# Attention phase of a four-phase layer: side work laid out tile by tile, projections split in two matmuls, head gather in six transfers with 8 KB runs

## What is computed

```python
def poincare_fully_connected(x, z, r, c):
    lam = 2.0 / (1.0 - c * sum(x * x, axis=-1))
    z_norm = maximum(norm(z, axis=0), EPS)
    inner = x @ (z / z_norm)
    v = 2.0 * z_norm / sqrt(c) * arcsinh(sqrt(c) * lam * inner * cosh(2cr) - (lam - 1.0) * sinh(2cr))
    w = sinh(sqrt(c) * v) / sqrt(c)
    return w / (1.0 + sqrt(1.0 + c * sum(w * w, axis=-1)))

xn = layernorm(x)                       # B=8 rows, T=1024, D=256
Q = poincare_fully_connected(xn, z_q, b_q, 1.0)
K = poincare_fully_connected(xn, z_k, b_k, 1.0)
V = xn @ w_v.T + b_v
probs = softmax(Qh @ Kh.T / 4)          # 16 heads of 16 columns
x = x + probs @ Vh
```

## Time and profile before

| what | value |
|---|---|
| median of 3 runs | 3177.55 us (3175.37 to 3177.95) |
| profiled execution, its own time | 3171.44 us |
| its span in the profile | 3169.6 us |
| mean granted TensorE clock | 0.962 of full |
| busy: PE, ACT, DVE, POOL | 2838.4, 2026.5, 1846.0, 1273.0 us |
| exponentials of `phase_b`, first and last start | 1449.0 and 2769.2 us |

### The profile page before, as it was taken

One profiled execution on the slowest core, in us unless ns is written; L12 is line 12 of the kernel. 1 busy time (PEld: TensorE's weight loads), 2 busy tenths in 40 slices (PEclk: granted clock), 3 DMA queues, 4 the chain that ended last, 5 costly groups with the idle time before them and its releaser, 6 DMA issues. The chain is left out here.

```text
span 3169.6 us, 38539 instructions
## 1 busy us (share of the span) xinstructions
PE 2838.4 (90%) x12161; PEld 1226.5 (39%) x12161; DVE 1846.0 (58%) x2420; ACT 2026.5 (64%) x2650; POOL 1273.0 (40%) x786
## 2 busy tenths in 40 slices
PE   3899999999979999657999999999999999969997
PEld 1455555555554444322323232323233332234443
DVE  8899999999973453454443444444444441144444
ACT  6454555455425555325889797978878889835554
POOL 4798899889861220141314131322313230021210
PEclk7899999999999999778999999999999999989999
DMA  2010001010012211206263635535553627231112
GB/s 80 1 37 27 30 26 36 23 33 26 24 56 75 80 53 53 67 11 132 29 146 42 134 54 94 93 73 92 92 94 58 116 46 128 27 114 48 60 53 67
DMA packets 163998, 200.30 MB, mean 63 GB/s; under 512 B 16504, under 2 KB 118272, under 8 KB 163840
## 3 DMA queue, kind: packets, MB, share of 16 engines
q1 hardware_dynamic: 163840, 198.25, 28.4%
HBM read 139.49 MB, written 58.72 MB: 63 GB/s over the span
## 5 line engine op out<-in xcount | busy, mean ns | idle before, releaser
L1859 ACT ACTIVATE b_pr<-b_ps 128x1024 f32<-128x1024 f32 x1024 | 1002.8, 1025 | 255.5 <-PE b_ps L1956 251.2
L1956 PE MATMUL b_ps<-b_st 128*128 128x512 bf16 x2048 | 591.2, 386 | 71.0 <-DMA b_st<-b_scratch 31.6
L1938 PE MATMUL b_acc<-b_pr,b_vaug 128*32 128x512 f32 x4096 | 549.0, 608 | 0.4 <-ACT b_pr L1859 0.4
L1956 PEld LDWEIGHTS b_ps<-b_st 128*128 128x128 bf16 x2048 | 150.3, 98 | 649.5 <-ACT b_pr L1859 381.9
L1257 PE MATMUL f_po<-f_s,f_w 128*128 128x512 f32 x768 | 355.0, 605 | 9.4 <-DVE f_xr L1042 5.9
L1030 DVE TENSOR_TENSOR f_turned<-f_cs,f_s 128x1024 f32<-128x1024 f32 x96 | 119.3, 1243 | 364.4 <-ACT f_cs L1159 359.4
L635 PE MATMUL a_pv<-a_xnT,a_wv 128*128 128x512 f32 x512 | 251.2, 614 | 52.8 <-DVE a_mem L403 38.7
L1123 ACT ACTIVATE f_h<-f_po,f_b 128x512 f32<-128x512 f32 x192 | 131.9, 687 | 218.1 <-PE f_po L1257 218.1
L627 PE MATMUL a_pu<-a_xnT,a_wk 128*128 128x512 f32 x512 | 238.3, 609 | 29.2 <-DVE a_frac L355 23.2
L1575 POOL TENSOR_TENSOR b_SQ<-b_A 128x1024 f32<-128x1024 f32 x32 | 64.7, 2021 | 467.1 <-DVE b_A L1672 467.1
L674 PE MATMUL a_py<-a_wo,a_out 128*128 128x256 f32 x960 | 229.1, 382 | 0.0
(11 more groups left out here) (259 smaller groups left out, 4694.4 us busy)
## 6 DMA issues: line engine op xcount, KB each, us to landing
b_st<-b_scratch SPq DMA_DIRECT2D x512, 128.0 KB, 7.0
b_scratch<-b_parts SPq DMA_DIRECT2D x32, 768.0 KB, 7.7
f_xl<-x SPq DMA_DIRECT2D x16, 1024.0 KB, 5.5
f_xr<-x SPq DMA_DIRECT2D x16, 1024.0 KB, 6.8
a_xl<-in_L_attn_a_x_dram SPq DMA_DIRECT2D x16, 512.0 KB, 4.2
x<-a_xr SPq DMA_DIRECT2D x32, 256.0 KB, 2.2
x<-f_xr SPq DMA_DIRECT2D x8, 1024.0 KB, 4.5
b_xl<-x SPq DMA_DIRECT2D x8, 1024.0 KB, 7.8
```

What stands on the lines that cost most here:

```text
L1859: nc.scalar.activation(pr[:, 4 * (blk % 2) + j, :], ps[:, j % 2, :], ACT.Exp, scale=SC).then_inc(S["probs_done"], 1)
L1938: x = nc.tensor.matmul(acc[32 * j:32 * j + 32, h * 512:(h + 1) * 512], vaug[:, kt, c:c + 32], pr[:, 4 * (kt % 2) + j, h * 512:(h + 1) * 51 ...
L1956: x = nc.tensor.matmul(ps[:, j % 2, h * 512:(h + 1) * 512], st[:, g % 2, 1, j, kt * P:(kt + 1) * P], st[:, g % 2, 0, j, h * 512:(h + 1) * ...
```

## The change

- **Layout of side work.** The table names single tiles with the unit after which they stand. Two-tile kinds (`inT`, `lamb`, `facb`, `out`) are split in their halves, which may stand in different blocks. A projection tile becomes `proja` and `projb`, one matmul each, after units 0 and 2. ACT steps carry a unit too, and are mostly one to a block. Preparations for the row after next (`stats`, `rstd`, `lam`, `inT`, `lamb` and projection tile 0) now stand in blocks 10 to 31 of the row before; `PROLOGUE` gains those of row 1, and `lam` has a buffer of its own (`dgl`).
- **Order of Q and K columns.** ScalarE permutes the weights once (`zp`), so that a partition of Q or K is (g, d, j) and not (g, j, d); the biases are loaded in that order in eight transfers instead of four.
- **Gather.** `b_scratch` is laid out as [Q or K, part, g, d, j, T]. Each gather is six transfers with 8 KB runs in place of sixteen with 2 KB runs: for Q one part repeated 3, 3 and 2 times (a broadcast of the source), for K parts 0 to 2, 0 to 2 and 0 to 1. The store keeps 2 KB runs.
- **Order on SP.** The load of `xl` comes first in a row, ahead of the gather of group 1.

```diff
-Q_PART = [0, 0, 0, 1, 1, 1, 2, 2]
-K_PART = [0, 1, 2, 0, 1, 2, 0, 1]
+Q_RUNS = [(0, 3, 0), (3, 3, 1), (6, 2, 2)]
+K_RUNS = [(0, 3, 0), (3, 3, 0), (6, 2, 0)]
...
 STEPS = {
-    1: [("inT", 0, 1)],
-    2: [("out", 3, -1), ("inT", 1, 1)],
-    3: [("lamb", 0, 1)], 4: [("proj", 0, 1), ("proj", 1, 1), ("vaug", 3, 0)], 5: [("proj", 2, 1)], 6: [("square", 0, 1), ("proj", 3, 1)],
-    7: [("root", 0, 1), ("y", 0, 1), ("v", 0, 1)], 8: [("ln", 0, 1), ("square", 1, 1), ("proj", 4, 1)],
-    9: [("up", 0, 1), ("root", 1, 1), ("y", 1, 1), ("proj", 5, 1)],
-    10: [("out", 0, 0), ("down", 0, 1), ("v", 1, 1)],
-    11: [("sign", 0, 1), ("ln", 1, 1), ("square", 2, 1), ("proj", 6, 1)],
-    12: [("up", 1, 1), ("root", 2, 1), ("y", 2, 1), ("proj", 7, 1)], 13: [("down", 1, 1), ("v", 2, 1)],
-    14: [("sign", 1, 1), ("ln", 2, 1), ("square", 3, 1), ("v", 3, 1)],
-    15: [("up", 2, 1), ("root", 3, 1), ("y", 3, 1), ("v", 4, 1), ("pair", 0, 1)],
-    16: [("down", 2, 1), ("v", 5, 1)], 17: [("sign", 2, 1), ("ln", 3, 1), ("up", 3, 1), ("sum", 0, 1)],
-    18: [("out", 1, 0), ("down", 3, 1)], 19: [("sign", 3, 1)], 20: [("pair", 1, 1), ("v", 6, 1)],
-    21: [("sum", 1, 1)], 22: [("fac", 0, 1), ("v", 7, 1)], 23: [("facb", 0, 1), ("split", 0, 1)],
-    24: [("facb", 1, 1)], 25: [("split", 2, 1)], 26: [("out", 2, 0)], 27: [("split", 1, 1), ("vaug", 0, 1)],
-    28: [("split", 3, 1), ("stats", 0, 2)], 29: [("vaug", 1, 1), ("rstd", 0, 2)], 30: [("lam", 0, 2)], 31: [("vaug", 2, 1)]}
+    0: [("proja", 1, 1, 0), ("projb", 1, 1, 2)], 1: [("proja", 2, 1, 0), ("projb", 2, 1, 2)],
+    2: [("square", 0, 1, 0), ("proja", 3, 1, 0), ("projb", 3, 1, 2)],
+    3: [("root", 0, 1, 0), ("proja", 4, 1, 0), ("y", 0, 1, 0), ("projb", 4, 1, 2)],
+    4: [("square", 1, 1, 0), ("ln", 0, 1, 2), ("proja", 5, 1, 0), ("vaug", 3, 0, 0), ("projb", 5, 1, 2)],
+    5: [("root", 1, 1, 0), ("up", 0, 1, 2), ("proja", 6, 1, 0), ("y", 1, 1, 0), ("projb", 6, 1, 2)],
+    6: [("square", 2, 1, 0), ("down", 0, 1, 2), ("proja", 7, 1, 0), ("projb", 7, 1, 2)],
+    7: [("ln", 1, 1, 0), ("out", 6, -1, 0), ("out", 7, -1, 2)],
+    8: [("root", 2, 1, 0), ("sign", 0, 1, 0), ("v", 0, 1, 0), ("y", 2, 1, 0)],
+    9: [("up", 1, 1, 0), ("v", 1, 1, 0)],
+    10: [("square", 3, 1, 0), ("v", 2, 1, 0), ("stats", 0, 2, 0)],
+    11: [("down", 1, 1, 0), ("v", 3, 1, 0), ("rstd", 0, 2, 0)],
+    12: [("ln", 2, 1, 0), ("v", 4, 1, 0), ("sign", 1, 1, 0)],
+    13: [("root", 3, 1, 0), ("v", 5, 1, 0), ("y", 3, 1, 0), ("out", 0, 0, 2), ("lam", 0, 2, 0)],
+    14: [("up", 2, 1, 0), ("v", 6, 1, 0), ("pair", 0, 1, 0), ("out", 1, 0, 2)],
+    15: [("down", 2, 1, 0), ("v", 7, 1, 0)], 16: [("ln", 3, 1, 0), ("sum", 0, 1, 0), ("sign", 2, 1, 0)], 17: [("up", 3, 1, 0)],
+    18: [("down", 3, 1, 0), ("out", 2, 0, 2)], 19: [("sign", 3, 1, 0), ("out", 3, 0, 2)],
+    20: [("pair", 1, 1, 0), ("sum", 1, 1, 2)], 21: [("fac", 0, 1, 0)],
+    22: [("facb", 0, 1, 0), ("facb", 1, 1, 2)], 23: [("facb", 2, 1, 0), ("split", 0, 1, 0)], 24: [("facb", 3, 1, 0)],
+    25: [("inT", 0, 2, 0), ("split", 2, 1, 0)], 26: [("inT", 1, 2, 0), ("out", 4, 0, 2)],
+    27: [("inT", 2, 2, 0), ("vaug", 0, 1, 0), ("out", 5, 0, 2)], 28: [("inT", 3, 2, 0), ("split", 1, 1, 0)],
+    29: [("lamb", 0, 2, 0), ("vaug", 1, 1, 0)], 30: [("lamb", 1, 2, 0), ("split", 3, 1, 0)],
+    31: [("proja", 0, 2, 0), ("projb", 0, 2, 2), ("vaug", 2, 1, 0)]}
...
-UNIT_OF = {1: (2,), 2: (0, 2), 3: (0, 1, 3), 4: (0, 1, 2, 3)}
-N_TILES = {"inT": 2, "lamb": 2, "proj": 1, "v": 1, "sum": 1, "facb": 2, "out": 2}
+    "stats0 rstd0 lam0 inT0 inT1 inT2 inT3 lamb0 lamb1 proja0 projb0 proja1 projb1 square0 proja2 projb2 proja3 projb3 "
...
+    [(step[:-1], int(step[-1]), 1) for step in "inT0 inT1 inT2 inT3 lamb0 lamb1 proja0 projb0".split()]
+TILE_KINDS = ("inT", "lamb", "projb", "v", "sum", "facb", "out")
+PE_KINDS = TILE_KINDS + ("proja",)
+ACT_KINDS = ("square", "root", "ln", "up", "down")
...
-    scratch = nc.dram_tensor("b_scratch", [2, 3, D, T], BF16, kind="Internal").ap()
+    scratch = nc.dram_tensor("b_scratch", [2, 3, H // 4, DK, 4, T], BF16, kind="Internal").ap()
...
+        zp = s.sb("zp", [P, 2, KD, D])
...
+        dgl = s.sb("dgl", [P, NT, P])
...
-        N_W = 16 * 8
-        N_G = 16 * 16
...
+        N_W = 16 * 12
+        N_G = 16 * (len(Q_RUNS) + len(K_RUNS))
...
-                sp.dma_start(scratch[o, :, f * P:(f + 1) * P].rearrange("w p t -> p w t"), parts[:, o, :, f, :])\
+                sp.dma_start(scratch[o, :, 2 * f:2 * f + 2].rearrange("w g d j t -> (g d j) w t"), parts[:, o, :, f, :])\
...
-            for o, part in enumerate((Q_PART, K_PART)):
-                for i, w in enumerate(part):
-                    sp.dma_start(st[i * DK:(i + 1) * DK, slot, o],
-                                 scratch[o, w, 64 * g:64 * g + 64, :].rearrange("(h d) t -> d h t", d=DK))\
-                        .then_inc(st_loaded[slot], 16)
+            for i, n, w in Q_RUNS:
+                sp.dma_start(st[i * DK:(i + n) * DK, slot, 0].rearrange("p h t -> p (h t)"),
+                             scratch[0, w, g].rearrange("d h t -> d (h t)").unsqueeze(0).broadcast_to([n, DK, 4 * T]))\
+                    .then_inc(st_loaded[slot], 16)
+            for i, n, w in K_RUNS:
+                sp.dma_start(st[i * DK:(i + n) * DK, slot, 1].rearrange("p h t -> p (h t)"),
+                             scratch[1, w:w + n, g].rearrange("w d h t -> w d (h t)")).then_inc(st_loaded[slot], 16)
...
-                    for f in range(KD):
-                        sp.dma_start(rcol[:, 2 * o + f:2 * o + f + 1],
-                                     r[f * P:(f + 1) * P].rearrange("(p o) -> p o", o=1)).then_inc(S["w_loaded"], 16)
+                    for g in range(G):
+                        c = 2 * o + g // 2
+                        sp.dma_start(rcol[g % 2 * 64:g % 2 * 64 + 64, c:c + 1],
+                                     r[64 * g:64 * g + 64].rearrange("(j d) -> d j", d=DK),
+                                     allow_slow_non_contiguous=True).then_inc(S["w_loaded"], 16)
...
+                    if left > 1:
+                        sp.wait_ge(S["inT_done"], b + 2)
+                        sp.sem_inc(passed, 1)
+                        sp.dma_start(xl[:], dram(xi, b + 2)).then_inc(S["xl_loaded"], 16)
...
-                    if left > 1:
-                        sp.wait_ge(S["inT_done"], b + 2)
-                        sp.sem_inc(passed, 1)
-                        sp.dma_start(xl[:], dram(xi, b + 2)).then_inc(S["xl_loaded"], 16)
...
+                        nc.gpsimd.tensor_tensor(dgl[:], eye, lam.unsqueeze(2).broadcast_to([P, NT, P]), ALU.mult)\
                             .then_inc(S["dlam_done"], 1)
...
+                nc.scalar.activation(zp[:].rearrange("p o k (g d j) -> p (o k g) d j", g=G, d=DK),
+                                     z_sb[:].rearrange("p o k (g j d) -> p (o k g) d j", g=G, d=DK), ACT.Copy).then_inc(S["z_done"], 1)
...
-                        steps = [x for x in steps_at(blk, first, left) if x[0] in ("square", "root", "ln", "up", "down")]
                         for j in range(4):
-                            for kind, i, off in steps[j // 2:j // 2 + 1] if j % 2 == 0 else ():
-                                step(kind, i, b + off)
+                            for kind, i, off, at in steps_at(blk, first, left):
+                                if kind in ACT_KINDS and at == j:
+                                    step(kind, i, b + off)
                             n = 4 * BLK * b + 4 * blk + j
...
-                    if kind == "proj":
...
+                    if kind in ("proja", "projb"):
+                        k = 0 if kind == "proja" else 1
+                        if k == 0:
+                            bank_free(m)
+                            if i == 0:
+                                pe.wait_ge(S["misc_taken"], m - 2)
                         q, c = i // 2, slice((i % 2) * 512, (i % 2 + 1) * 512)
-                        for k in range(KD):
-                            x = nc.tensor.matmul(bank, z_sb[:, q // 2, k, (q % 2) * P:(q % 2 + 1) * P], xnT[:, k, c],
-                                                 start=k == 0, stop=k == KD - 1)
+                        x = nc.tensor.matmul(bank, zp[:, q // 2, k, (q % 2) * P:(q % 2 + 1) * P], xnT[:, k, c],
+                                             start=k == 0, stop=k == KD - 1)
+                        if k == 0:
+                            return
                     if kind == "v":
                         bank_free(m)
                         for k in range(KD):
...
-                            for q, (kind, i, off, h) in enumerate(tiles):
-                                if UNIT_OF[len(tiles)][q] == j:
+                            for kind, i, off, at in steps_at(blk, first, left):
+                                if kind in PE_KINDS and at == j:
                                     if kind == "out":
-                                        out(G * (b + off) + i, m - h, par - h, h)
```

(64 more changed lines are left out.)

108 lines of the change are left out of this document (51 added, 57 removed), and 5 rows, old and new, of the table PROLOGUE.

## The result

| | before | after |
|---|---|---|
| median, same chip | 3176.46 us (3174.16 to 3177.95, 4 runs) | 3320.99 us (3314.82 to 3323.33, 4 runs) |
| ratio | | 1.0453, 95% interval 1.0435 to 1.0471 |
| span of the profiled execution | 3169.6 us | 3318.8 us |
| exponentials, first and last start | 1449.0 and 2769.2 us | 1474.1 and 2918.3 us |

A forecast was written before the change was run, and what follows sets the result against it. PE bounds, ACT has some 30 us to spare. Rows add 81 us, the first gather 16.3 and setup 2: 3171.4 + 99 = 3271 profiled, median 6.1 above, 3277; own range 3235 to 3310, 8 in 10 within 3215 to 3400.

The forecast's parts named there:

- slow-run rival: Gather: 8 KB runs are slower on one engine; at 20 GB/s a gather takes 41 us, total about 3437; chance 0.14.
- Number of engines: Gather: outermost counts 3, 3 and 2 leave three or two engines; the first two get all six transfers, 31.4 us.
- The first rival: Gather: all engines carry it after all, in 7 to 16.6 us; total 3151; chance 0.12.
- Length of a gather: Each gather, from issue to landing: 31.4 us on the first two engines and 1.5 on top, 32.9 us.
- The sum of 3225: Whole kernel: with some 27 GiB/s an engine, the gather takes 27 + 1.5 us and the total ends at about 3225.
- Group 1: Gather issued at 12.6 us into a row, landed at 45.5, wanted at 46.6: no wait, 1 us in hand.
- Group 2: Gather behind the store and load of `xr` lands at 87.9 us into a row, wanted at 87: 2.0 late with restart.
- Block 0: First block of a row runs at a low clock and holds a projection: 2.5 us more.
- Row 7: Last row, no side work: waits of 6.9 us before block 8 and 6 before block 16, 154 in all.
- Layout: New order of side work: 162.8 us for 32 blocks against 166.3, 3.5 a row, 24.5 over seven rows.
- The jump: Row borders: the hardware loop's jump, 3 to 5 us at four of seven, now hides in the wait for the gather.
- Setup: Before row 0: four more small loads and the permuting copy +2 us (0 to 4); row 1's `PROLOGUE` steps hide in the wait.

The follow-up runs named there:

- e1_gather16: The changed kernel with each gather cut into sixteen transfers of 16 rows, runs still 8 KB: 3156.66 us, 0.9953 to the kernel before.
- e11_store_held: The changed kernel with SP waiting for a row's first gather to land before storing the second half of the parts: 3306.03 us, 1.0429 to the kernel before.
- e4_proj_whole: The changed kernel with sixteen transfers to a gather, and both halves of every projection behind unit 2: 3161.89 us, 0.9957 to the kernel before.
- e2_gather_alone: The kernel before with only the changed gather (permuted weights, new scratch layout, six transfers): 3327.69 us, 1.0493 to the kernel before.
- e5_layout_alone: The changed kernel with the gather, scratch and biases of before and no permutation: 3150.32 us, 0.9944 to the kernel before.

## Why the forecast was right, and which terms were off

The mechanism was right but for one wait: engines by the outermost count, a wait of PE for `b_st` at every row's start, a small one before block 16, none at group 3, rows 0 to 6 longer. It had no wait at group 1, and there is one. It was 44 us under the median, which lies 11 us above the forecast's own range of 3235 to 3310 and inside that of 8 in 10 only because the latter took in half of the slow-run rival; in the profiled execution 149.2 us lie between the spans where the terms summed to 99, so 50 are to be found. Blocks are measured as in the forecast, from one first exponential to the next, and a row from its first to that of the next row.

| term | forecast, us | measured, us |
|---|---|---|
| ahead of and in the setup | +2 | +6.1 |
| first gather, issue to exponential | +16.3 | +19.0 |
| row 0 | 175.3 | 179.1 |
| rows 1 to 6, mean | 178.8 | 185.3 |
| row 7 | 154 | 154.2 |

The differences are 4.1, 2.7, 3.8, 6 x 6.5 and 0.2: 49.8.

- **Number of engines: right.** Three are busy (0.19), then two: the counts 3, 3, 2 give the first two engines 96 runs and the third 64, and the step from 74 to 49 GB/s comes after about seven tenths of the time. Never more than three are busy though six transfers are queued, so all of them begin with the same engines, which the prediction had taken without a row. The rival of slow long runs (20 GB/s an engine, 41 us a gather) is out: an engine moves 25 to 27 GB/s once under way. In the mean of the gather alone it is 23.6 (96 runs in 34.8 less 1.5 us), so a part of the overrun goes that rival's way. The Trainium skill's rule ("DMA: Bandwidth & Descriptors", "Why a DMA increments its semaphore by 16 and not by 1": the largest count up to 16 that divides both slowest counts) holds for all three shapes tried: 3, 2 and 48 rows. The first rival, all engines after all, did not happen, but its price was right: 3151 worked out, 3157 measured where `e1_gather16` makes it so.
- **Length of a gather: the term that was mis-sized.** 32.9 forecast; by itself 34.8 ahead of row 0 and 35.7 in the mean of the borders, and 35.5 to 38.4 with what SP issues behind it: 1437.44 to 1474.09 less 1.1 is 35.6 before row 0, 2173.81 to 2210.61 is 36.8 between rows 3 and 4, 37.1 the mean. The 2 to 3 us of the first kind are, as far as the DMA view shows, the slower first 8 us and the one engine that ends late; the 1.4 us of the second are the store of the other half and the load of x, which `e11_store_held` takes out. The sum of 3225 that stands beside the forecast, for a faster engine, is further off. Block 31 lasts 21.2 us in the mean of rows 1 to 6, against 5.65 + 11.5 forecast: +4.0.
- **Group 1: "no wait, 1 us in hand".** With a gather 3.6 us longer there is one. Issued at 2039.02, row 3's ends PE's idle time at 2075.51:

```profile
2039.02 2.14 SPq L1474 DMA_DIRECT2D b_st<-b_scratch  x3
```

```profile
2075.51 0.95 PE L1978 MATMUL b_ps<-b_st 128*128 128x512 bf16 x2 [2.55 <-DMA b_st<-b_scratch]
```

  That is 36.5 us. Blocks 7 and 8 grow by 2.0 us in the mean of six rows.
- **Group 2: near.** SP stores `xr` 45.9 us into row 2 (forecast 47) and issues the gather 51.9 into it (51.5). Blocks 15 and 16 together are 2.9 us above those of the layout alone, 2.0 forecast (whose landing at 87.9 is 0.8 more than its terms add up to: 47 + 4.5 + 2.7 + 32.9 = 87.1). Row 3 has no such wait: it lost 4.3 us at group 1, which moved the demand back, so the two waits are to be taken together. Row 6 has none either, with 1.6 us at group 1.
- **Block 0: right.** 7.6 us, against 5.65 + 2.5.
- **Row 7: right by luck.** Its waits are 10.3 us at group 1 and 7.0 at group 2, 6.9 and 6 forecast; the rest of the row is 136.9 us, where 154 less these two waits left 141.1. The two misses, 4.4 and 4.2 us, cancel.
- **Layout: near, for a reason I had half.** Written out, a middle row is 163.2 us (162.8 forecast) against 165.4 (166.3), so 2.2 and not 3.5 us. Row 6 gains 6.3 and row 0 2.9 instead. In all 20.3 us by the exponentials with the loop left in, where 24.5 were forecast; 17.8 by the ratio. `e4_proj_whole` shows no part of the split of the projections in it (the intervals are 5 us to either side); whether it is the filling of the empty blocks alone was not tried.
- **The jump: right, but not to nothing.** In the change, block 31 of rows 1 to 4 is 21.3 us in the mean with the loop and 21.1 without, so its pause is hidden as forecast. Still 10 us go by the ratios (whose intervals overlap at the edge) and 15 by the medians. In the profiled executions 2.9 are ahead of row 0; in rows 1 to 4 the waits before block 16 fall from 13.8 us in sum to 2.7, while those at group 1 grow from 8.9 to 13.2. Why the first of the two waits is longer there and the sum of both smaller stays open; I had called this hidden whole.
- **Setup.** The phase itself begins 2.5 us later than before, and its way to the first gather is 3.6 longer (110.5 to 114.1). `e2_gather_alone`, with the permutation and the four loads alone, has 111.9; `e5_layout_alone`, with the longer `PROLOGUE` alone, 111.4. So the permutation and the loads are 1.4, near the 2 forecast, and the new steps of row 1 do not all fall into the wait as forecast. The 2.5 us at the start no edit explains. In the profiled executions of this study that start lies anywhere from 1320.7 to 1326.9 us.

The sum of a middle row: 178.8 + 4.0 (block 31) + 2.0 (group 1) + 0.9 (group 2) - 0.6 (block 0) + 0.4 (layout) = 185.5, against 185.3. The prediction's last sign of being wrong, a PSUM bank held by DVE in blocks 3 to 8, did not come: the list of waits has none of PE in `phase_b` that ends by DVE's taking a `pm` tile.

## What to carry to other kernels

Fewer and larger transfers are no gain in themselves: look at the outermost count of source and destination before merging. A repeat or a part index of 3 put there tied a transfer to three engines, and several such transfers queued on the same ones. Such a gather is priced by the engine with the most runs; here that came 2 to 3 us short of the gather alone, and what was issued behind it added 1.4. Where a forecast leaves 1 us in hand, the demand is not covered. And a pause that ends by "issue" at the border of a hardware loop is worth writing the loop out once: it gave 0.9% here, more than the layout.

## What had not been expected of the hardware

- Runs of 8 KB brought nothing over runs of 2 KB when a gather writes 16 rows at a time: 137 against 141 GB/s, all engines busy in both. With 48 rows at a time it was 211.
- A gather on three engines starts slowly: 57 to 66 GB/s for 8 us, then 74 to 90.
- Transfers into 16 rows hold up others beside them: while K went in its eight transfers, Q and K together had 142 GB/s, and most of Q was still ahead. That it is the destination's rows that limit is read from 142 against 211 GB/s, not seen engine by engine.
- The jump of a hardware loop costs 5.4 us at a row's border and 1.6 us in the block behind it, which begins at a low clock, and the code written out five times over showed no cost: rows 1 to 5 of the layout alone last 163.2 us each.
